# VectorE takes only the moments of a norm's tiles; GpSimd joins the halves and makes mean, variance and root

## The reference, cut to what matters

```python
def _layernorm(x, axis=-1, eps=1e-05):
    m = jnp.mean(x, axis=axis, keepdims=True)
    v = jnp.var(x, axis=axis, keepdims=True)
    return (x - m) / jnp.sqrt(v + eps)

x = x + _layernorm(attention(_layernorm(x), Wq, Wk, Wv, Wo))      # norms "x" and "a"
x = x + _layernorm(ternary_linear(_layernorm(x), weight, alpha, bias))  # norms "y" and "f"
```

## Time and profile before

| what | value |
|---|---|
| median of 3 runs | 1683.8 us (1673.1 to 1694.15) |
| the profiled execution | 1686.89 us, span 1684.8 us |
| busy share of the span | PE 88%, DVE 83%, ACT 74%, POOL 38% |
| granted TensorE clock, mean | 0.948 of full speed |
| chain that ended last | PE 52%, DVE 30%, issue 10%, ACT 3%, DMA 3%, POOL 2% |
| one turn of the loop (two halves) | about 197 us |

### The profile page before, as it was taken

The page is one execution under the profiler, slowest core; times in us unless marked ns, Lnnn a source line. Parts: engine busy times, 40 slices in busy tenths (PEclk is TensorE's granted clock), DMA queues, the critical chain, the costliest instruction groups (busy, mean ns, idle before and its releaser), DMA issues.

```text
span 1684.8 us, 38037 instructions
## 1 busy us (share of the span) xinstructions
PE 1483.1 (88%) x11994; PEld 496.9 (29%) x11994; DVE 1402.8 (83%) x1899; ACT 1248.8 (74%) x2485; POOL 639.6 (38%) x703
## 2 busy tenths in 40 slices
PE   4589999989999899998999999998999999899973
PEld 3223332223333233322323233232333333222222
DVE  3698898887989789887998989897898999999904
ACT  1058888877888678786788878886787888888861
POOL 1034045261634526162361616335261633423230
PEclk8579999999999899998999999998999999999995
DMA  2310302113020311212112130202102130211010
GB/s 94 90 42 19 97 19 68 40 40 89 25 79 15 94 40 35 66 31 75 42 48 51 33 106 21 82 15 91 41 27 77 31 78 14 74 27 40 14 44 15
DMA packets 72793, 85.45 MB, mean 51 GB/s; under 512 B 17552, under 2 KB 58384, under 8 KB 71056
## 3 DMA queue, kind: packets, MB, share of 16 engines
q1 hardware_dynamic: 72592, 82.86, 17.6%
HBM read 46.66 MB, written 24.64 MB: 42 GB/s over the span
## 4 chain that ended last, share of the span: by engine, by line
PE 52%; DVE 30%; issue 10%; ACT 3%; DMA 3%; POOL 2%; SPq 0%; DVEq 0%; ACTq 0%; POOLq 0%
DVE row_max L1047 21%; PE pv L863 19%; PE smax L841 18%; PE ring L946 3%; PE ring L885 3%; PE ring L934 2%; PE ring L952 2%; PE ring L927 2%; ACT heads L792 2%; DVE sf_bn L1030 1%; DVE sy_bn L1030 1%; PE ring L906 1%; ACT probs L746 1%; DVE sx_bn L1030 1%; DVE max_parts L1065 1%
## 5 line engine op out<-in xcount | busy, mean ns | idle before, releaser
L1047 DVE TENSOR_REDUCE row_max<-smax 128x1 f32<-128x1024 f32 x1024 | 1211.4, 1217 | 171.9 <-PE smax L841 163.5
L746 ACT ACTIVATE probs<-ring 128x512 f32<-128x512 f32 x2048 | 1108.9, 597 | 266.3 <-PE ring L885 254.1
L841 PE MATMUL smax<-k_rows,q_rows 48*128 48x512 f16 x2048 | 633.6, 393 | 96.8 <-DVE row_max L1047 82.7
L885 PE MATMUL ring<-q_rows,k_rows 50*128 50x512 f16 x2048 | 643.6, 388 | 6.2 <-DMA q_rows<-max_rows 6.1
L863 PE MATMUL pv<-probs,v_cols 128*32 128x256 f32 (+1 forms) x6120 | 610.0, 471 | 24.7 <-ACT heads L792 24.3
L841 PEld LDWEIGHTS smax<-k_rows,q_rows 48*128 48x128 f16 x2048 | 123.4, 94 | 602.2 <-DVE row_max L1047 359.3
L863 PEld LDWEIGHTS pv<-probs,v_cols 128*32 128x32 f32 x6120 | 121.8, 108 | 309.9 <-issue 180.7
L885 PEld LDWEIGHTS ring<-q_rows,k_rows 50*128 50x128 f16 x2048 | 140.8, 94 | 57.2 <-ACT probs L746 38.2
L465 POOL TENSOR_TENSOR attnT<-pairs,inv_rows 128x512 f32<-128x512 f32 x31 | 39.4, 1270 | 303.8 <-DMA inv_rows<-inv_sums_dram 219.5
L356 POOL TENSOR_TENSOR sa_rs<-sa_ve,m_half 128x4 f32<-128x4 f32 x16 | 16.3, 1017 | 263.7 <-DVE sa_ve L1038 263.7
L946 PE MATMUL ring<-wo_sb,attnT 128*128 128x256 f32 x256 | 74.0, 415 | 13.0 <-DVE attnT L465 13.0
(11 more groups left out here) (130 smaller groups left out, 1038.9 us busy)
## 6 DMA issues: line engine op xcount, KB each, us to landing
q_stage_dram<-q_parts SPq DMA_DIRECT2D x48, 256.0 KB, 2.4
q_rows<-q_stage_dram SPq DMA_DIRECT2D x32, 384.0 KB, 5.5
x_in<-in_L_attn_x SPq DMA_DIRECT2D x8, 1024.0 KB, 6.8
pairs<-heads SPq DMA_DIRECT2D x64, 128.0 KB
inv_rows<-inv_sums_dram SPq DMA_DIRECT2D x32, 256.0 KB
res<-in_L_attn_x SPq DMA_DIRECT2D x16, 512.0 KB, 5.5
out<-res SPq DMA_DIRECT2D x16, 512.0 KB, 3.0
k_rows<-k_stage_dram SPq DMA_DIRECT2D x64, 96.0 KB, 4.0
```

The source lines that it names most:

```text
L746: eng.activation(probs[:, s % PSLOTS, j, :], ring[:, n % RING, :], ACT.Exp, scale=score_unit).then_inc(ring_read, 1)
L841: mm = eng.matmul(smax[:, side, c, :], q_rows[at:to, qc, kv * KVP + jp, qt * P:(qt + 1) * P], k_rows[at:to, kv, c * 512:(c + 1) * 512], st ...
L885: eng.matmul(ring[:, n % RING, :], k_rows[at:to, g, kt * P:(kt + 1) * P], q_rows[at:to, h.qc, g * KVP + j // 2, :], start=True, stop=True)\
L1047: eng.tensor_reduce(row_max[:, g % 2, at:at + 1], smax[:, side, :, :].rearrange("p c n -> p (c n)"), AX.X, ALU.max).then_inc(max_read, 1)
```

## The change: what it does

`moments` keeps only `bn_stats`. The semaphore of a norm counts its tiles and nothing else. `root`, on GpSimd, waits for all tiles and makes everything else for all tiles at once, from the six numbers per token: the sum and the difference of the two means and the sum of the two squared deviations (three instructions); minus half the sum of the means, the variance's first part with epsilon added, and half the difference (three); the square of that half difference (one); the sum of the two parts of the variance (one); then the power -0.5, as before. Between these groups GpSimd waits for its own results (semaphore `joined`). Nothing else is changed; the steps at which things are due are the same.

```diff
--- before.py
+++ after.py
@@ -109,6 +109,7 @@
 ROT_ALL = sum(ROT_OPS)
 SPLIT_OPS = (2, 2, 2)
 SPLIT_ALL = sum(SPLIT_OPS)
+JOIN_OPS = 8
 SPLIT_ACT = 3 * DT
 
 
@@ -250,7 +251,7 @@
 
             return (sb(f"{name}_bn", [P, n, 6], F32), sb(f"{name}_mv", [P, n, 2], F32),
                     sb(f"{name}_nm", [P, n], F32), sb(f"{name}_ve", [P, n], F32),
-                    sb(f"{name}_rs", [P, n], F32))
+                    sb(f"{name}_rs", [P, n], F32), sem(f"{name}_joined"))
 
         st_x, st_a, st_y, st_f = stats("sx", KT), stats("sa", ST), stats("sy", ST), stats("sf", ST)
 
@@ -351,13 +352,31 @@
 
         def root(eng, st, n, mom, norm, nth):
 
-            _, _, _, ve, rs = st
-            eng.wait_ge(mom, (nth + 1) * (2 * n + 2))
+            bn, mv, nm, ve, rs, joined = st
+            at = nth * JOIN_OPS
+            eng.wait_ge(mom, (nth + 1) * n)
+            eng.sem_inc(passed, 1)
+            eng.tensor_tensor(mv[:, :, 0], bn[:, :, 1], bn[:, :, 4], ALU.add).then_inc(joined, 1)
+            eng.tensor_tensor(mv[:, :, 1], bn[:, :, 1], bn[:, :, 4], ALU.subtract).then_inc(joined, 1)
+            eng.tensor_tensor(ve[:, :], bn[:, :, 2], bn[:, :, 5], ALU.add).then_inc(joined, 1)
+            eng.wait_ge(joined, at + 3)
+            eng.sem_inc(passed, 1)
+            eng.tensor_scalar(nm[:, :], mv[:, :, 0], -0.5, None, ALU.mult).then_inc(joined, 1)
+            eng.tensor_scalar(ve[:, :], ve[:, :], 1.0 / D, EPS, ALU.mult, ALU.add).then_inc(joined, 1)
+            eng.tensor_scalar(mv[:, :, 1], mv[:, :, 1], 0.5, None, ALU.mult).then_inc(joined, 1)
+            eng.wait_ge(joined, at + 6)
+            eng.sem_inc(passed, 1)
+            eng.tensor_tensor(mv[:, :, 1], mv[:, :, 1], mv[:, :, 1], ALU.mult).then_inc(joined, 1)
+            eng.wait_ge(joined, at + 7)
+            eng.sem_inc(passed, 1)
+            eng.tensor_tensor(ve[:, :], ve[:, :], mv[:, :, 1], ALU.add).then_inc(joined, 1)
+            eng.wait_ge(joined, at + 8)
+            eng.sem_inc(passed, 1)
             eng.tensor_tensor(rs[:, :], ve[:, :], m_half[:, 0:n], ALU.pow).then_inc(norm, 1)
 
         def normalise(eng, dst, src, st, n, norm, nth, per):
 
-            _, _, nm, _, rs = st
+            _, _, nm, _, rs, _ = st
             eng.wait_ge(norm, RAISED + nth * per + 1)
             eng.sem_inc(passed, 1)
             for t in range(n):
@@ -1022,20 +1041,11 @@
                 eng.tensor_tensor(wf_tern[:, :, :], wf_tern[:, :, :], wf_neg[:, :, :], ALU.subtract)\
                    .then_inc(w_prep, 1)
 
-            def moments(src, st, n, mom, nth, t, tiles):
-
-                bn, mv, nm, ve, _ = st
-                at = nth * (2 * n + 2)
+            def moments(src, st, mom, t, tiles):
+
+                bn = st[0]
                 for i in range(t, t + tiles):
                     eng.bn_stats(bn[:, i, :], src[:, i, :]).then_inc(mom, 1)
-                if t + tiles == n:
-                    eng.wait_ge(mom, at + n)
-                    eng.sem_inc(passed, 1)
-                    for i in range(n):
-                        eng.bn_aggr(mv[:, i, :], bn[:, i, :]).then_inc(mom, 1)
-                    eng.wait_ge(mom, at + 2 * n)
-                    eng.tensor_scalar(nm[:, :], mv[:, :, 0], -1.0, None, ALU.mult).then_inc(mom, 1)
-                    eng.tensor_scalar(ve[:, :], mv[:, :, 1], EPS, None, ALU.add).then_inc(mom, 1)
 
             def due(s, when):
 
@@ -1086,7 +1096,7 @@
                             if now[0] == 0:
                                 eng.wait_ge(x_loaded, (h.mom + 1) * 16)
                                 eng.wait_ge(x_norm, RAISED + h.mom * (KT + 1))
-                            moments(x_in, st_x, KT, x_mom, h.mom, *now)
+                            moments(x_in, st_x, x_mom, *now)
                     if h.pro is not None and h.alone:
                         between(eng, h, s)
                     if h.epi is not None:
@@ -1101,17 +1111,17 @@
                                 eng.wait_ge(a_norm, RAISED + nth_epi * (ST + 2))
 
                             eng.wait_ge(ring_read, h.done("WO", now[0] + now[1] - 1))
-                            moments(act, st_a, ST, a_mom, nth_epi, *now)
+                            moments(act, st_a, a_mom, *now)
                         if now := due(s, Y_MOM):
                             if now[0] == 0:
                                 eng.wait_ge(a_norm, RAISED + (nth_epi + 1) * (ST + 2))
                                 eng.wait_ge(y_norm, RAISED + nth_epi * (ST + 1))
-                            moments(res, st_y, ST, y_mom, nth_epi, *now)
+                            moments(res, st_y, y_mom, *now)
                         if now := due(s, F_MOM):
                             if now[0] == 0:
                                 eng.wait_ge(biased, (nth_epi + 1) * ST)
                                 eng.wait_ge(f_norm, RAISED + nth_epi * (ST + 2))
-                            moments(act, st_f, ST, f_mom, nth_epi, *now)
+                            moments(act, st_f, f_mom, *now)
             schedule(half, eng, prepare)
```

## The result

| what | before | after |
|---|---|---|
| median of the runs on the same chip | 1681.91 us (1673.1 to 1694.15) | 1731.42 us (1729.68 to 1731.78, 4 runs) |
| ratio, with its 95% interval | | 1.028 [1.023, 1.033] |
| span of the profiled execution | 1684.8 us | 1729.5 us |
| mean granted TensorE clock | 0.948 | 0.929 |
| busy share of the span: PE, DVE, ACT, POOL | 88, 83, 74, 38% | 87, 79, 72, 42% |

The change makes the kernel slower by about 47 us (0.028 of 1682). The forecast was 1701, 17 us above the kernel before; 1731 lies inside its range, near the upper end.

A forecast was written before the change was run, and what follows sets the result against it. Neither TensorE nor VectorE was taken to bound everywhere; they take turns. Terms of +2.9, +18 for clock dips and -4 for spared dips made +17 on 1686.9, or 1704; 3 us lower at the median, 1701 us, range 1666 to 1737.

The forecast's parts named there:

- The order of engines in the x halves: Six loop halves with norm x: GpSimd's sum, then norms x and y run late, TensorE stops 3.6 us at transposes HT.
- J: Length of GpSimd's eight tiny instructions and four waits per norm, ahead of the root: 1.9 us, bounds 1.3 to 3.5.
- the gain of the other halves: Six halves (1, 0) to (6, 0), without norm x: transposes HT reached 1.1 us earlier, -6.6 us in all.
- The dip: Half-speed TensorE clock behind the stop at transposes HT: 3 us in each of six halves, +18 us.
- SP's list: Norm f's store, residual load and move of heads, queued together: +0.3 us per half with norm x, +1.8 in all.
- The second norm x: Ahead of the first half's end: the change gives -1.3 us.
- Halves (6, 1) to (7, 1): Last three halves: norms a and y gain 1.4 to 1.6 each, norm f's lateness offsets some: -2.1 us.
- the -4 for spared dips: Some TensorE stops of 1.3 us, shortened to 0.5, may spare short clock dips: two of 2 us, -4.
- The end: Norm f of (7, 1) and three norms behind the last half, alone on the path: 1.1 us each, +4.4.
- Tiny instructions twice VectorE's: Rival: GpSimd's tiny instructions take twice VectorE's time, so J is 3.5 and the kernel 1746 us; chance 0.18.
- Full return: Rival: VectorE's saved time comes back in full, decided at J of 0.7 in halves with norm x: 1650 us; chance 0.05.
- The clock holds: Rival: no half-speed clock behind the stops at transposes HT, so the forecast without its 18 us: 1683; chance 0.13.

The follow-up runs named there:

- experiment 5: Changed kernel with SP moving the first pair of heads before waiting for norm f's store and loading the residual: 1727.0 us, ratio 1.025.
- Experiment 3: Changed kernel with joins on GpSimd only in the loop's twelve halves, on VectorE everywhere else: 1712.9 us, ratio 1.018.
- experiment 4: Changed kernel with only norm x's aggregates, means and variances back on VectorE: 1706.1 us, ratio 1.010.
- experiments 8: Kernel before with only norm f in the loop joined on GpSimd: 1685.8 us, ratio 1.001.
- 9: Kernel before with SP's list turned, heads first and residual later: 1678.5 us, ratio 0.997.
- experiment 10: Kernel before with only norm x of the loop joined on GpSimd, at step 27 instead of 15: 1691.2 us, ratio 0.999.
- 11: Kernel before with norm f in the loop joined on GpSimd and SP moving heads ahead of the residual load: 1685.6 us, ratio 0.999.
- Experiment 6: Changed kernel with a two-instruction join from the even elements alone, a probe that leaves out the odd ones: 1669.8 us, ratio 0.992.

## Why the prediction was too low, step by step

The forecast added 17 us and the profiled executions differ by 44.7. The order of engines in the x halves came out as written. What failed is above all the price of the four halves outside the loop, +1.9 in the forecast and +23.0 measured; then the length of the join, J = 1.9 against 2.47; and the gain of the other halves, -6.6 against nothing.

**What bounds, and the mechanism: right.** The order of engines in the half with norm x was the argument, and each step of it is in the trace after: the sum later, the join of x straight behind it, norm y last, TensorE waiting at HT, the half clock behind the stop. That these halves measured 26.4 us, just as forecast, is partly luck, though. HT is 3.55 later, not 1.9: three joins of 0.57 more than forecast are the missing 1.7. The dip cost about 2.0, not 3. SP's list does make VectorE's reciprocal wait 0.4 to 0.9 us behind them, but where this wait is gone (experiment 5) the stretch is no shorter, so its 0.3 is nothing; and 1.05 instead of 0.8 came back behind norm f. An error of 1.65 up and several small ones down cancel.

**J: mis-sized.** Taken 1.9, measured 2.47, so above the forecast's own 1.7 to 2.4. The per-instruction length was guessed by carrying a fit of 256 and 512 elements down to none, 184 ns, which is near (208 ns in the mean). The overlap was wrong: a group of three was taken as 0.4 us in all, and the two groups last 0.51 and 0.81, since those with constants start 0.27 to 0.32 apart. That is 0.52 of the missing 0.57. The four waits were right (0.74 against 0.76).

**The four halves outside the loop: the larger failure.** They were forecast at -0.4 - 2.1 + 4.4 = +1.9 and measured +23.0. Experiment 3 puts these joins alone back and leaves +1.0. Three steps failed in them:
- *The second norm x*, "-1.3": its moments stand at the same place in VectorE's list and end 2.8 us later, and its root starts 4.4 us later than before (2.8 from the moments, 1.6 from the join). TensorE waits 3.52 us at the transposes of the next row, where it waited 0.81. With this norm back on VectorE the start is +1.0 (experiment 4). I had this norm end ahead of a half without asking what waits for it.
- *Halves (6, 1) to (7, 1)*, "what is late by 1.1 is late there": right in kind, but 1.1 turned into 2.8. The reciprocal waits 4.09 where it waited 1.33, and TensorE 4.32 behind it, and a dip of 6.8 us is recorded at each of the four stops of 2.4 to 4.3 us here. Experiment 5 takes the queue away and the three halves are 0.8 shorter than before (1.6 longer than with the same edit in the kernel before).
- *Norm y there*: VectorE's moments of y wait for norm a's sum, and TensorE stops behind that. After, half (7, 0):

```profile
1531.45 0.75 DVE L1048 BATCH_NORM_STATS2 sy_bn<-res 128x6 f32<-128x256 f32 x2 [1.77 <-POOL res L448]
...
1533.38 0.39 PE L860 MATMUL smax<-k_rows,q_rows 48*128 48x512 f16 x1 [2.42 <-DVE row_max L1057]
```

The prediction saw this wait in the x halves only, where GpSimd was late anyway, and not where nothing hides it. It is left in experiment 5 too.

**The other halves of the loop, "-6.6": failed, no gain.** From norm a to norm f four of them are as long as before to a tenth; the two that gained 2.3 are those whose short dip of 3.4 us, at 336 and 732 us, is gone. So the -4 for spared dips fits and the -6.6 does not. How far the change spares them is open: the seven profiles with norms a and y joined on GpSimd at J of 0.7 or 2.47 have no dip between norms a and f in these halves, but the five with both on VectorE have two, none, one, four and three (before, experiments 8, 9, 10, 11). GpSimd's norm y was said to be "just in time". With J at 2.47 it is not, and TensorE waits for it:

```profile
549.81 0.44 PE L959 MATMUL ring<-ident,act 128*128 128x128 f32 x2 [0.46 <-POOL act L383]
```

Experiment 6 shows that a short join brings HT 1.0 forward here, as the step said, and that 0.8 of it is lost again where VectorE's split, 1.2 us in place of 0.36, falls beside the rotation of K. The kernel after loses 0.9 of VectorE's time at the same place; that this and the wait of 0.46 use up the whole gain is argued, not shown.

**The end: near**, +5.7 against +4.4. Each of the four roots starts 1.7 to 1.8 later behind its moments, not 1.1; of these 6.9 us, 5.7 reach the path (0.9, 1.8, 1.2 and 1.8).

**The rivals.** "Tiny instructions twice VectorE's" priced J = 3.5 at 1746, nearer to 1731 than the forecast, but not by its reason: these instructions take 208 ns on GpSimd in the mean against VectorE's 170, 1.2 times as long, and J is 2.47. GPSIMD Engine Reference of the Trainium skill, section Engine selection, calls GpSimd about twice as slow for two inputs. The trace agrees at 512 elements (1270 against 693 ns) and does not at four, as far as its rows go: VectorE has no two-input row of four elements, and its one row of a single element took 154 ns. "Full return" had its point at J of 0.7: experiment 6 has J = 0.70 and stands at 1670, not 1650. Its x halves gained 1.7 to norm f and 0.9 behind it, as written (2.6), so the direction and the point are right, while the other halves of the loop and its turns returned 1 us instead of 11. "The clock holds" is excluded by the dips.

**How time goes with J.** Three kernels with all joins on GpSimd: J = 0.70 gives 0.992, 2.47 gives 1.028, and about 4.9 gives 1.12 (1884.9 / 1687.0). That is 35 us per microsecond of J up to 2.47 (61 us by 1.77) and about 60 beyond (from two runs), as the joins of the other halves come onto the path too. The forecast had 28 (45 us by 1.6). With J = 2.47 from the start it would have said 1717.

Open: why the start of experiment 5 is 2 us longer than the kernel after, and how the turns of the loop, of which one alone is 3.6 longer after and 7.5 longer in experiment 10, choose between a short and a long dip. The runs of one kernel vary by up to 28 us (the kernel before, 1672.6 to 1700.7 on one chip), and that is why gains of 5 us were not to be told here.

## What to carry to other kernels

Cutting work from a busy engine helped here only where no other engine's list was longer at that place. Write down the receiving engine's list between two waits in the half that is fullest, and put the moved chain into it, with its latency and not its busy time: eight instructions of 0.2 us were 2.5 us. Then walk every other place where the same code runs (ahead of the loop, the last halves, the turn), since four halves of sixteen lost as much as the whole loop did. Ask of each queue behind the moved step what it gives its next consumer, because 1.8 us late at a root became 2.8 us at a DMA's consumer and a stop of 4.3 on TensorE. A stop of that length can cost twice, once as a stop and again as a dip behind it, which was worth 2.0 to 2.3 us here.

## What the runs showed of the hardware that was not expected

- A two-input add or multiply of GpSimd on four elements per partition is busy 0.20 to 0.21 us. Without a wait between them such instructions start 0.15 apart, and those with constants 0.27 to 0.32 apart; VectorE's two tiny ones are 0.17 and 0.16 long and start 0.08 apart in the kernel before.
- VectorE's tiny instructions, 0.17 us elsewhere, took 2.00 and 1.22 beside one of GpSimd's large ones (experiments 4 and 6) and ended 0.03 behind it. A change of timing on GpSimd can make VectorE slower without giving it work.
- In all six x halves a stop of 5.1 us on TensorE went with 6.8 us at the lower of the two clock levels, which began 0.8 to 2.2 us ahead of the stop's end; useless matmuls in the place of the stop (52 records) left the clock at 1.00. Behind a stop of 2.2 us the kernel of experiment 4 had no dip twice, 3.4 us once and 6.8 us three times.
